# Another order of the weight chunks, o's low-rank part on VectorE, low-rank rows split and stacked through DRAM

## Chip, cores and metric

One NeuronCore of a Trainium2 chip runs the whole program. The metric is the device time of one execution in microseconds (us), of which the median of several runs is given. Engines are named as in the profile: PE is TensorE, DVE is VectorE, ACT is ScalarE, POOL is GpSimd, SP is SyncE, which here only issues DMAs.

## What is computed

Four stages on a tensor of 1024 tokens by 512. The change touches the first. Its weights are NF4 codes (integers 0 to 15) with a scale for every 64 inputs, each with a low-rank addition:

```python
def _lin_lora(x, W, A, B):
    return x @ W.T + (x @ A.T) @ B.T          # rank 16
q, k, v = (_lin_lora(x, dequant(codes_attn[i], scales_attn[i]), A_h[i], B_attn[i]) for i in range(3))
attn = (q + k + v) / 3.0
o = _lin_lora(attn, dequant(codes_attn[3], scales_attn[3]), A_h[3], B_attn[3])
x1 = x + o
g = _lin_lora(x1, dequant(codes_gu[0], ...), A_h[4], B_gu[0])
u = _lin_lora(x1, dequant(codes_gu[1], ...), A_h[5], B_gu[1])
d = _lin_lora(silu(g) * u, dequant(codes_down, ...), A_down, B_down)
return x1 + d                                # then x = layernorm(x + this)
```

(The code above is the reference in short.) x is 2 x 512 x 512, the hidden width is 1792. After it come a quantised 512 x 512 layer with a rank 64 addition, an attention layer with one head of 128, and a layer of 64 rank-16 experts of which 16 are taken, each with a residual and a layer norm.

## The kernel before

Weights are handled in **chunks** of 128 x 512. `chunk_list` (L111) gives their order: four of o, then q, k, v of slice 0, of slice 1, 2, 3, then g and u of hidden tiles 0 and 1, d 0 and d 1, then g, u, d of the further tiles. A chunk is looked up from its codes by piecewise lines: ACT makes four planes (`low` two of them, L785; `mid`, L807; `out`, the top one, L785) and DVE joins them in four steps (L1316 low, L1322 mid, L1329 clip, L1338 value). POOL multiplies the value by its scale (L718, for q, k, v L723) into `wf`, a ring of three. Codes come through a ring of three as well: SP issues the code of chunk j only when the top plane of chunk j-3 is made (L658).

Since q, k, v and o are linear, they are folded: per slice i of 128 inputs the sum of the three weights is made in the PSUM bank `acc_ps` (low-rank products L1049, then fp32 products with a scaled unit matrix L1052, L1055), split by ACT and DVE into a high and a low part (`acc`; `wq_hi`, `wq_lo`), and multiplied with o's weight (`wo_hi`, `wo_lo`) in twelve matmuls plus three times the unit matrix (L1069). The result is the matrix `m1`, again split (`m1_hi` by ACT, `m1_lo` by DVE). `partial(i, r)` (L1027) adds slice i's share of x1 = m1 x for the first 512 tokens to bank r; the other 512 tokens follow as four products of twelve matmuls. All products are made in three matmuls, high x high, high x low, low x high (`product`, L991).

o's four chunks go through PE too: for each, the low-rank product (L1037) and an fp32 product with the unit matrix (L1040), whose bank ACT and DVE split.

x1 is split into `x1_hi`, `x1_lo` (ACT, DVE), and DVE adds it to x in `xs`. Then the **units**: unit n is a hidden tile f = n // 2 and a half b of the tokens, a gate and an up product of twelve matmuls each. For g, u and d chunks PE makes the low-rank product in the bank `lora_ps` (`lora`, L1000; the same bank as `acc_ps`, so each waits for `lora_added` of the one before), DVE adds it to `wf` (`merge`, L1353), ACT and POOL split (`split`: `gu_hi` L780, `gu_lo` L740). `res(t)` (L1137) transposes a token tile of xs, which ACT copies to `rows`; the down products are added there by DVE (L1413).

The low-rank rows of g and u lie in the 128 rows of `la_gu` and `lb_gu` three times over (high, low, high), so that one matmul gives all three products. They are loaded from DRAM already stacked; ACT makes the high part of all rows (`bprep`) and DVE the low part of one band (L1306). For d the same is `dprep`, after x1.

Each engine runs one hand-written order: `vector_order` (L135) for ACT, DVE and POOL together, in which `half(c, 0)` is mid and clip of a chunk and `half(c, 1)` is low of the next chunk and out; `tensor_order` (L251) for PE's units. Work that is queued behind a waiting instruction of its engine waits too.

## Time and profile before

| | |
|---|---|
| median of 3 runs | 535.43 us (533.67 to 535.5) |
| profiled execution, its own time | 534.0 us |
| its span | 532.1 us |
| mean granted clock of PE | 0.993 |
| PE matmul busy | 494.5 us (93%) |
| DVE busy | 379.4 us (71%) |
| ACT busy | 293.9 us (55%) |
| POOL busy | 251.6 us (47%) |

The profile is of one execution. Busy time is the time in which an engine has an instruction at work. The granted clock is a share of full speed, of PE alone. In a timeline each line is an instruction, or some merged of one kind: start, duration, engine and line, what it writes and reads, how many, and in square brackets how long the engine was idle before it and what it waited for. Ends of matmuls are modelled, so their starts are the safer numbers. A wait for several things is put down to the last to come.

### The profile page before, as it was taken

What the parts mean: (1) busy time and instruction counts of PE and PEld (TensorE: products, weight loads), DVE (VectorE), ACT (ScalarE), POOL (GpSimd) and SP (SyncE); (2) the same over time, 40 slices, a digit from 0 to 9 for tenths busy, and PEclk for the clock granted to TensorE, in tenths of its full rate; (3) what the DMA queues carried; (4) which work ended last, traced back from release to release, by engine and by line L of the source; (5) the groups of instructions that cost most, each with busy time, mean ns of one, the idle gap of its engine ahead of it and who ended that gap; (6) DMA issues with size and microseconds to landing.
All of it is one profiled execution on the core that took longest, in us unless ns stands there. A gap on an engine that the chain in (4) does not pass through costs nothing.

```text
span 532.1 us, 7568 instructions
## 1 busy us (share of the span) xinstructions
PE 494.5 (93%) x2278; PEld 394.7 (74%) x2278; DVE 379.4 (71%) x716; ACT 293.9 (55%) x541; POOL 251.6 (47%) x252
## 2 busy tenths in 40 slices
PE   2968999788999999999999999899998899999995
PEld 0236678567888888888888888688886788888874
DVE  4888898666789789797987983577457966366442
ACT  6688856676666576666674742158487422332021
POOL 3357702465566576665674753147479410110001
PEclk9999999899999999999999999999999999999998
DMA  6575421243233333343333300740000000000011
GB/s 169 173 263 159 139 59 41 79 139 100 80 106 75 96 105 118 82 119 97 105 115 97 103 19 0 267 155 5 1 1 1 2 2 19 21 20 22 0 41 39
DMA packets 21415, 43.01 MB, mean 81 GB/s; under 512 B 3328, under 2 KB 3456, under 8 KB 21120
## 3 DMA queue, kind: packets, MB, share of 16 engines
q1 hardware_dynamic: 21152, 42.15, 25.6%
q0 software_dynamic: 224, 0.38, 0.3%
q8 instruction: 19, 0.31, 0.2%
q14 instruction: 20, 0.16, 0.1%
HBM read 40.42 MB, written 2.10 MB: 80 GB/s over the span
## 4 chain that ended last, share of the span: by engine, by line
PE 69%; ACT 3%; issue 3%; DVE 2%; POOL 0%; POOLq 0%; ACTq 0%; DVEq 0%
PE bank L996 62%; PE bank L1162 3%; PE bank L1009 2%; PE bank L1266 1%; ACT prob L957 1%; ACT pT_hi L780 1%; PE bank L1018 0%; DVE rmax L1480 0%; DVE pT_lo L1306 0%; ACT eb_hi L780 0%; ACT bank L785 0%; DVE rows L1413 0%; POOL gu_lo L740 0%; ACT v_hi L780 0%; PE bank L1025 0%
## 5 line engine op out<-in xcount | busy, mean ns | idle before, releaser
L718 POOL TENSOR_TENSOR wf<-value,scale 128x512 f32<-128x512 f32 x50 | 64.5, 1290 | 93.1 <-DVE value L1338 93.1
L996 PE MATMUL bank<-x_hi,gu_hi 128*128 128x512 f32 x224 | 89.9, 401 | 1.7 <-POOL gu_lo L740 1.7
L996 PE MATMUL bank<-x_lo,gu_hi 128*128 128x512 f32 x224 | 88.2, 394 | 0.0
L996 PE MATMUL bank<-x_hi,gu_lo 128*128 128x512 f32 x224 | 88.1, 393 | 0.0
L763 POOL TENSOR_TENSOR rstd<-veps,neg_half 128x1 f32<-128x1 f32 x32 | 17.6, 549 | 121.8 <-issue 110.5
L785 ACT ACTIVATE bank<-code 128x512 f32<-128x512 int32 x124 | 68.7, 587 | 0.0
L1316 DVE SCALAR_TENSOR_TENSOR low<-bent,bank 128x512 f32<-128x512 f32 x62 | 42.5, 685 | 24.0 <-ACT bank L785 19.4
L746 POOL TENSOR_TENSOR h_lo<-act_f,h_hi 128x512 fp32r<-128x512 f32 x28 | 36.3, 1297 | 31.7 <-ACT h_hi L780 31.7
L1413 DVE SCALAR_TENSOR_TENSOR rows<-bank,rows 128x512 f32<-128x512 f32 x48 | 33.0, 688 | 24.7 <-PE bank L996 24.3
L996 PEld LDWEIGHTS bank<-x_hi,gu_hi 128*128 128x128 f32 x224 | 42.6, 190 | 9.9 <-issue 2.1
L996 PEld LDWEIGHTS bank<-x_hi,gu_lo 128*128 128x128 f32 x224 | 42.5, 190 | 9.1
L996 PEld LDWEIGHTS bank<-x_lo,gu_hi 128*128 128x128 f32 x224 | 42.6, 190 | 7.9
L1329 DVE SCALAR_TENSOR_TENSOR low<-low,bank 128x512 f32<-128x512 f32 x62 | 42.7, 688 | 6.9 <-DVE bank L1322 0.5
L780 ACT ACTIVATE h_hi<-act_f 128x512 fp32r<-128x512 f32 x28 | 17.7, 631 | 52.0 <-DVE act_f L1403 48.5
L996 PE MATMUL bank<-wd_hi,h_hi 128*128 128x512 f32 x112 | 44.2, 395 | 1.6 <-DVE rows L1413 1.6
L1322 DVE SCALAR_TENSOR_TENSOR bank<-code,bank 128x512 f32<-128x512 int32 x62 | 42.6, 686 | 1.6 <-ACT bank L807 1.6
L996 PE MATMUL bank<-wd_hi,h_lo 128*128 128x512 f32 x112 | 43.7, 390 | 0.0
L996 PE MATMUL bank<-wd_lo,h_hi 128*128 128x512 f32 x112 | 43.7, 390 | 0.0
L1338 DVE SCALAR_TENSOR_TENSOR value<-bank,low 128x512 f32<-128x512 f32 x62 | 42.4, 684 | 0.1
L785 ACT ACTIVATE bent<-code 128x512 f32<-128x512 int32 x62 | 38.5, 621 | 3.2 <-DMA code<-codes 3.2
L740 POOL TENSOR_TENSOR gu_lo<-wf,gu_hi 128x512 fp32r<-128x512 f32 x28 | 36.7, 1310 | 5.2 <-ACT gu_hi L780 4.8
L918 ACT ACTIVATE rows<-rows,nbias,rstd 128x512 f32<-128x512 f32 x24 | 19.3, 812 | 35.7 <-POOL nbias L766 35.6
(198 smaller groups left out, 1172.7 us busy)
## 6 DMA issues: line engine op xcount, KB each, us to landing
code<-codes SPq DMA_DIRECT2D x62, 256.0 KB, 2.7
scale<-scales SPq DMA_DIRECT2D x100, 128.0 KB, 3.0
xs<-xT SPq DMA_DIRECT2D x2, 1024.0 KB, 5.6
ea_raw<-ex_A SPq DMA_DIRECT2D x1, 2048.0 KB, 9.9
eb_raw<-ex_B SPq DMA_DIRECT2D x1, 2048.0 KB, 7.5
out<-rows SPq DMA_DIRECT2D x8, 256.0 KB, 2.0
bgu_raw<-loB_gu SPq DMA_DIRECT2D x1, 896.0 KB, 4.7
wqkv_raw<-w_qkv SPq DMA_DIRECT2D x1, 768.0 KB, 4.3
```

Of the source, the lines that this page charges most:

```text
L718: pool.tensor_tensor(w, v, scale[:, i % RING_CODES, :], ALU.mult).then_inc(scaled_done, 1)
L740: pool.tensor_tensor(lo, shaped(c, w), hi.bitcast(F32), ALU.subtract).then_inc(lo_done, 1)
L746: pool.tensor_tensor(h_lo[:, f % RING_H, hs], act_f[:, n % 2, :], h_hi[:, f % RING_H, hs].bitcast(F32), ALU.subtract).then_inc(hlo_done, 1)
L780: nc.scalar.activation(dst, src, ACT.Copy).then_inc(done, 1)
L785: nc.scalar.activation(dst, src, ACT.Prelu, bias=float(start), scale=float(slope), alpha=float(alpha)).then_inc(done, 1)
L918: nc.scalar.activation(rows[:, t, :], src, ACT.Identity, bias=nbias[:, s:s + 1], scale=rstd[:, s:s + 1]).then_inc(norm_done, 1)
L996: last = nc.tensor.matmul(ps, a, b, start=start and i == 0 and n == 0, stop=stop and i == len(terms) - 1 and n == 2)
L1316: nc.vector.scalar_tensor_tensor(low[:, j % 2, :], bent[:, j % 2, :], float(BEND_LOW[3] - BEND_LAST[3]), last_ps[:, :], ALU.add, ALU.min). ...
L1322: nc.vector.scalar_tensor_tensor(mid_ps[:, :], code[:, j % RING_CODES, :], float(CODE_SHIFT), mid_ps[:, :], ALU.add, ALU.max).then_inc(mid ...
L1329: nc.vector.scalar_tensor_tensor(lj, lj, float(BEND_LAST[3]), mid_ps[:, :], ALU.add, ALU.min)\
L1338: nc.vector.scalar_tensor_tensor(value[:, j % 2, :], top_ps[:, :], float(BEND_TOP[3]), low[:, j % 2, :], ALU.add, ALU.max).then_inc(value_ ...
L1413: nc.vector.scalar_tensor_tensor(rows[:, t, :], down_bank(gi, t)[:, :], 1.0 / GAIN, rows[:, t, :], ALU.mult, ALU.add).then_inc(down_added, 1)
```

## The change

- **Order of the chunks.** q, k, v of slice 0, then the four of o, then q, k, v of slices 1 to 3, then as before. In `vector_order` the first sixteen chunks take fixed extras ahead of clip, ahead of out and after out, from three tables.
- **o.** The four low-rank products of o run after slice 0's, ahead of slice 0's sums, and end in their own banks. The products with the unit matrix are gone. DVE adds the low-rank product to `wf` (`merge`), and ACT and POOL split it as they do for g. m1 of slice 0 has its own bank, and m1 is scaled by 1 / (3 GAIN).
- **Scaled unit matrices** are made by POOL instead of ACT, and the scales of q, k, v come through SP's queue behind the first code instead of POOL's.
- **x.** It is loaded in eight tiles, each with its own semaphore, ahead of the codes of o 3 to k 3.
- **Low-rank rows of g, u, d.** They are loaded once each, spread over 128 partitions (576 and 352 columns), split there by ACT and POOL (`spread`), written to DRAM as high and low, and read back into the stacked rows: `stack_gu` (2 stores, a wait, 9 loads) ahead of v 3's code, `stack_d` (2 stores, a wait, 12 loads) ahead of g 1's. The stacked buffers are zeroed first (DVE, POOL). `bprep` and `dprep` are gone.
- **x1 and rows.** `xs` now gets x1 alone, by ACT for tiles other than 5 and 7 and by DVE for these. `rows` is loaded with x ahead of d 1's code, and DVE adds the transposed x1 to it (`res`), which ACT copied before.
- **Low-rank products of g and u.** g 0 after the first partial of slice 3, u 0 after the last, g 1 and u 1 after the second and third product of the other tokens. The res steps begin one place later.

```diff
-    chunks = [("o", k) for k in range(KT)] + [(m, i) for i in range(KT) for m in "qkv"]
+    chunks = [(m, 0) for m in "qkv"] + [("o", k) for k in range(KT)]
+    chunks += [(m, i) for i in range(1, KT) for m in "qkv"]
...
+X1F_ON_V = (5, 7)
+
+BEFORE_CLIP = {
+    ("o", 2): [("acc", 0)], ("o", 3): [("merge", ("o", 1)), ("split", ("o", 1))],
+    ("q", 1): [("merge", ("o", 2)), ("split", ("o", 2))],
+    ("q", 2): [("m1", 0)], ("k", 2): [("acc", 1)], ("k", 3): [("acc", 2)],
+}
+BEFORE_OUT = {
+    ("o", 2): [("merge", ("o", 0)), ("split", ("o", 0))], ("q", 1): [("merge", ("o", 3))],
+    ("v", 2): [("m1", 1)], ("v", 3): [("m1", 2)],
+}
+AFTER_OUT = {
+    ("q", 1): [("split", ("o", 3))], ("k", 1): [("xsplit", 0)], ("v", 1): [("spread", 0)], ("q", 2): [("xsplit", 1)],
+    ("k", 2): [("spread", 1)], ("v", 2): [("xsplit", 2)], ("q", 3): [("xsplit", 3)], ("v", 3): [("xsplit", 4)],
+}
...
+        c = CHUNKS[j]
+        order.append(("mid", c))
+        order += BEFORE_CLIP.get(c, [])
+        order += [("clip", c), ("low", CHUNKS[j + 1])]
+        order += BEFORE_OUT.get(c, [])
+        order.append(("out", c))
+        order += AFTER_OUT.get(c, [])
...
+    order += [("acc", 3), ("xsplit", 5)]
+    half(("u", 0), 0)
     due.clear()
-    order += [("acc", 2 * KT - 1), ("bprep", 0), ("bprep", 1), ("m1", KT - 1)]
-    half(("u", 0), 0)
+    order.append(("xsplit", 6))
     half(("u", 0), 1)
     due.clear()
-    order += [("x1", 0), ("x1", 1), ("x1", 2), ("x1", 3), ("merge", ("g", 0)), ("x1", 4), ("split", ("g", 0))]
+    order += [("m1", 3), ("xsplit", 7)]
     half(("g", 1), 0)
-    order += [("x1", 5), ("merge", ("u", 0))]
+    order += [("x1", 0), ("merge", ("g", 0)), ("split", ("g", 0)), ("x1", 1), ("x1", 2), ("x1", 3)]
     half(("g", 1), 1)
-    order += [("x1", 6), ("split", ("u", 0)), ("x1", 7), ("dprep", 0)]
+    order += [("merge", ("u", 0)), ("split", ("u", 0)), ("x1", 4)]
+    due.clear()
     half(("u", 1), 0)
+    order += [("x1", 5), ("merge", ("g", 1)), ("split", ("g", 1))]
     half(("u", 1), 1)
+    order += [("x1", 6), ("merge", ("u", 1)), ("split", ("u", 1)), ("x1", 7)]
+    due.clear()
     half(("d", 0), 0)
-    order += [("silu", 0), ("res", 0)]
+    order.append(("silu", 0))
     half(("d", 0), 1)
     unit_h(0)
-    order.append(("res", 1))
+    order.append(("res", 0))
     half(("d", 1), 0)
-    order += [("silu", 1), ("res", 2)]
+    order += [("silu", 1), ("res", 1)]
     half(("d", 1), 1)
     unit_h(1)
-    order.append(("res", 3))
+    order.append(("res", 2))
...
+            def stack_gu():
+
+                sp.wait_ge(spreadhi_done, 1)
+                sp.wait_ge(spreadlo_done, 1)
+                sp.wait_ge(zeroed_v, 2)
+                cols = spread_cut(0)
+                sp.dma_start(scratch_hi[:, cols], spread_hi[:, cols].bitcast(F32)).then_inc(scratch_in, 16)
+                sp.dma_start(scratch_lo[:, cols], spread_lo[:, cols].bitcast(F32)).then_inc(scratch_in, 16)
+                sp.wait_ge(scratch_in, 32)
+                for i in range(3):
+                    a, b = (scratch_lo if i == 1 else scratch_hi), (scratch_lo if i == 2 else scratch_hi)
+                    for g in range(2):
+                        r = 32 * i + RANK * g
+                        sp.dma_start(long(la_gu[r:r + RANK, g, :].bitcast(F32)), wide(a[64 * g:64 * g + 64, 0:P]))\
+                            .then_inc(gu_rows_in, 16)
+                    sp.dma_start(long(lb_gu[32 * i:32 * i + 32, :].bitcast(F32)), wide(b[:, P:SPREAD_GU])).then_inc(gu_rows_in, 16)
...
+            def stack_d():
+
+                sp.wait_ge(spreadhi_done, 2)
+                sp.wait_ge(spreadlo_done, 2)
+                sp.wait_ge(zeroed_p, 2)
+                piece = FF // 2 // PIECES
+                cols = spread_cut(1)
+                sp.dma_start(scratch_hi[:, cols], spread_hi[:, cols].bitcast(F32)).then_inc(scratch_in, 16)
+                sp.dma_start(scratch_lo[:, cols], spread_lo[:, cols].bitcast(F32)).then_inc(scratch_in, 16)
+                sp.wait_ge(scratch_in, 64)
+                for i in range(3):
+                    a, b = (scratch_lo if i == 1 else scratch_hi), (scratch_lo if i == 2 else scratch_hi)
+                    for g in range(2):
+                        r, half = 64 * g + RANK * i, slice(64 * g, 64 * g + 64)
+                        sp.dma_start(long(la_dp[r:r + RANK, :].bitcast(F32)), wide(a[half, SPREAD_GU:SPREAD_GU + piece]))\
+                            .then_inc(d_rows_in, 16)
+                        sp.dma_start(long(lb_dp[r:r + RANK, g, :].bitcast(F32)), wide(b[half, SPREAD_GU + piece:]))\
+                            .then_inc(d_rows_in, 16)
...
+                if c in x_before:
+                    k, tk = x_tile(x_before[c])
+                    sp.dma_start(xs[:, k, tk], xT[:, k, tk]).then_inc(x_in[x_before[c]], 16)
+                if c == ("q", 2):
+                    sp.dma_start(spread[:, spread_cut(0)], lora_gu).then_inc(spread_in[0], 16)
+                    sp.dma_start(spread[:, spread_cut(1)], lora_d).then_inc(spread_in[1], 16)
+                if c == ("v", 3):
+                    stack_gu()
+                if c == ("g", 1):
+                    stack_d()
+                if c == ("d", 1):
+                    sp.wait_ge(gu_rows_in, 16 * 9)
+                    sp.wait_ge(d_rows_in, 16 * 12)
+                    for b in range(NB):
+                        sp.dma_start(rows[:, b * TPB:(b + 1) * TPB, :], x_rows[:, b * TPB:(b + 1) * TPB, :])\
+                            .then_inc(x_rows_in, 16)
...
+                    if n not in X1F_ON_V:
+                        act.wait_ge(xlo_done, KT * (b + 1))
+                        copy(xs[:, o, b * SEQ:(b + 1) * SEQ], mm_ps[n % 4][:, :], x1f_done)
...
+            pe.wait_ge(lora_in, 32)
+            slice_lora(0)
+            pe.wait_ge(olora_in, 32)
+            for k in range(KT):
+                nc.tensor.matmul(mm_ps[k][:, :], la_o[:, k * P:(k + 1) * P], lb_o[:, :], start=True, stop=True)\
+                    .then_inc(olora_ready, 1)
+            pe.wait_ge(gain_set, 3)
+            slice_sums(0)
+            pe.wait_ge(acchi_done, 1)
+            pe.wait_ge(acclo_done, 1)
+            slice_lora(1)
+            slice_m1(0)
+            for i in range(1, KT):
+                if i > 1:
+                    pe.wait_ge(m1hi_done, i)
+                    pe.wait_ge(m1lo_done, i)
+                    slice_lora(i)
+                slice_sums(i)
+                pe.wait_ge(m1hi_done, i)
+                pe.wait_ge(m1lo_done, i)
+                pe.wait_ge(xhi_done, i)
+                pe.wait_ge(xlo_done, i)
+                partial(i - 1, 0)
+                partial(i - 1, 1)
+                slice_m1(i)
+                partial(i - 1, 2)
+                partial(i - 1, 3)
...
+                if r == 0:
+                    lora(("g", 0))
+            lora(("u", 0))
 
             pe.wait_ge(xhi_done, 2 * KT)
             pe.wait_ge(xlo_done, 2 * KT)
             for n in range(KT, NB * KT):
                 r = n - KT
-                pe.wait_ge(x1hi_done, n - 3)
-                pe.wait_ge(xs_done, n - 3)
+                pe.wait_ge(x1lo_done, n - 3)
+                pe.wait_ge(x1f_done, x1f_before(n - 3))
                 cut = slice(r * P, (r + 1) * P)
                 product(mm_ps[r][:, :], [(m1_hi[:, k, cut], m1_lo[:, k, cut], x_hi[:, k, SEQ:], x_lo[:, k, SEQ:])
                                          for k in range(KT)]).then_inc(x1_ready, 1)
-                if r in (1, 3):
-                    lora((("u", 0), ("g", 1))[r // 2])
+                if r in (1, 2):
+                    lora((("g", 1), ("u", 1))[r - 1])
...
+                    if c[0] == "o":
+                        dve.wait_ge(olora_ready, c[1] + 1)
+                        nc.vector.scalar_tensor_tensor(w, mm_ps[c[1]][:, :], GAIN, w, ALU.mult, ALU.add)\
+                            .then_inc(o_merged, 1)
+                        continue
...
+                elif kind == "res":
+                    t = item[1]
+                    dve.wait_ge(res_ready, t + 1)
+                    dve.wait_ge(x_rows_in, 16 * NB)
+                    nc.vector.tensor_tensor(rows[:, t, :], bank[7][:, :], rows[:, t, :], ALU.add).then_inc(res_set, 1)
```

## Rows read from the trace of the kernel before

**Rows 1.** Waits of PE up to 140 us; line waited for: us, times, longest

```profile
PE bank L1037 <- DMA lb_qkv<-loB_qkv: 10.2, 1, 10.2
PE bank L1052 <- POOL wf L728: 3.5, 1, 3.5
PE bank L1146 <- ACT rows L780: 3.5, 1, 3.5
...
PE bank L1009 <- DVE wf L1353: 1.8, 2, 1.4
PE bank L996 <- POOL gu_lo L740: 1.7, 1, 1.7
```

**Rows 2.** Busy time by engine in stretches; granted clock, DMA share, GB/s last

```profile
97.10:101.40 4.30, 4.27 (x17) 3.52 (x18) 3.21 (x6) 3.22 (x7) 1.64 (x3) 0.62 0.45 122
130.00:170.00 40.00, 40.00 (x188) 33.48 (x187) 33.51 (x51) 24.67 (x46) 23.57 (x18) 1.00 0.30 86
```

**Rows 3.** Timeline of PE; start, duration, instruction, idle before and releaser

```profile
10.19 2.07 PE L1037 MATMUL bank<-lb_o,la_o 16*128 16x512 f32 x2 [10.19 <-DMA lb_qkv<-loB_qkv]
12.19 2.08 PE L1040 MATMUL bank<-wf,unit_eye 128*128 128x512 f32 x2
...
26.22 2.07 PE L1049 MATMUL bank<-la_qkv,lb_qkv 48*128 48x128 f32 x8
...
37.12 0.77 PE L996 MATMUL bank<-wo_hi,wq_hi 128*128 128x512 f32 x1 [1.50 <-DVE wq_lo L1306]
...
71.84 0.47 PE L996 MATMUL bank<-x_hi,m_hi 128*128 128x512 f32 x1
```

**Rows 4.** Timeline of PE later; first gate product, ninth product

```profile
87.53 0.44 PE L996 MATMUL bank<-x_hi,gu_hi 128*128 128x512 f32 x1
...
127.39 0.47 PE L996 MATMUL bank<-x_hi,gu_hi 128*128 128x512 f32 x1 [1.75 <-POOL gu_lo L740]
```

**Rows 5.** Timeline of DVE; start, duration, instruction, idle before and releaser

```profile
5.03 0.69 DVE L1316 SCALAR_TENSOR_TENSOR low<-bent,bank 128x512 f32<-128x512 f32 x1 [3.84 <-ACT bank L785]
...
18.94 0.69 DVE L1306 TENSOR_TENSOR wo_lo<-bank,wo_hi 128x512 fp32r<-128x512 f32 x1 [0.26 <-ACT wo_hi L780]
...
28.02 0.69 DVE L1316 SCALAR_TENSOR_TENSOR low<-bent,bank 128x512 f32<-128x512 f32 x1 [0.37 <-ACT bank L785]
28.62 0.68 DVE L1338 SCALAR_TENSOR_TENSOR value<-bank,low 128x512 f32<-128x512 f32 x1
...
30.61 0.68 DVE L1316 SCALAR_TENSOR_TENSOR low<-bent,bank 128x512 f32<-128x512 f32 x1
...
61.21 0.69 DVE L1338 SCALAR_TENSOR_TENSOR value<-bank,low 128x512 f32<-128x512 f32 x1
...
68.88 2.02 DVE L1306 TENSOR_TENSOR lb_gu<-bgu_raw,lb_gu 32x1792 fp32r<-32x1792 f32 x1 [0.38 <-ACT lb_gu L780]
71.05 0.69 DVE L1367 SCALAR_TENSOR_TENSOR m_lo<-bank,m_hi 128x512 fp32r<-128x512 f32 x1
```

**Rows 6.** Timeline of ACT in the o chunks

```profile
18.31 0.60 ACT L780 ACTIVATE wo_hi<-bank 128x512 fp32r<-128x512 f32 x1 [1.37 <-PE bank L1040]
18.80 0.62 ACT L785 ACTIVATE bent<-code 128x512 f32<-128x512 int32 x1
19.32 1.11 ACT L785 ACTIVATE bank<-code 128x512 f32<-128x512 int32 x2
```

**Rows 7.** Timeline of SP's DMA issues

```profile
28.90 0.43 SPq L644 DMA_DIRECT2D bgu_raw<-loB_gu  x1
29.37 0.42 SPq L645 DMA_DIRECT2D agu_raw<-loA_gu  x1
```

**Rows 8.** DMA issues by tile; KB each, median us from issue to landing

```profile
code<-codes SPq DMA_DIRECT2D x62, 256.0 KB, 2.7
...
out<-rows SPq DMA_DIRECT2D x8, 256.0 KB, 2.0
```

**Rows 9.** Waits of SP's queue, whole span

```profile
SPq L658 <- ACT bank L785: 125.1, 58, 6.7
```

More of the change, by code:

```diff
@@ L124 @@
 MERGED = [c for c in CHUNKS if c[0] not in "qkvo"]
-SPLIT = MERGED
+SPLIT = [c for c in CHUNKS if c[0] not in "qkv"]
 SCALED = [c for c in CHUNKS if c[0] not in "qkv"]
@@ L155, in half @@
         if part == 1:
-            if c[0] == "o":
-                due.append([3, ("acc", c[1])])
-            elif c[0] == "v":
-                due.append([3, ("acc", KT + c[1])])
-                due.append([6, ("m1", c[1])])
-            elif c[0] not in "qk":
-                due.append([2, ("merge", c)])
-                due.append([3, ("split", c)])
+            due.append([2, ("merge", c)])
+            due.append([3, ("split", c)])
         due.sort(key=lambda x: x[0])
@@ L591, in weight_wait, with x_tile, spread_cut, x1f_before @@
             engine.wait_ge(scaled_done, CHUNKS.index(c) + 1)
-        def acc_bank(a):
-            return mm_ps[a] if a < KT else acc_ps
-        def acc_dest(a):
-            hi, lo = (wo_hi, wo_lo) if a < KT else (wq_hi, wq_lo)
-            return hi[:, a % KT, :], lo[:, a % KT, :]
+        def x_tile(i):
+            return i % KT, slice(i // KT * SEQ, (i // KT + 1) * SEQ)
+        def spread_cut(i):
+            return (slice(0, SPREAD_GU), slice(SPREAD_GU, SPREAD_GU + SPREAD_D))[i]
+        def x1f_before(n):
+            return sum(i not in X1F_ON_V for i in range(n))
+        def m1_bank(i):
+            return mm_ps[3] if i == 0 else acc_ps
         def dest(c):
             kind, k = c
+            if kind == "o":
+                return wo_hi[:, k, :], wo_lo[:, k, :]
             if kind in "gu":
```

267 lines of the change are left out of this document (109 added, 158 removed).

## The prediction

> **What bounds the kernel now.** I read the waits of PE first, because PE is busy 93% of the span, and then the stretches. From 130 us on PE has no gap (40.00 of 40.00 us busy in the stretch from 130 to 170, at granted clock 1.00 [rows 2]), while DVE is at 33.5. What the change touches lies ahead of that, so a microsecond taken from the time at which PE enters that unbroken stretch is a microsecond off the end. The waits of PE up to 140 us are the stock to draw on [rows 1]: 10.2 for the first low-rank rows, 3.5 for a summed slice, and in the unit stage 3.5 (a transpose of xs waiting for ACT's copy of rows), 1.8 (two low-rank products waiting for a merge) and 1.7 (gu_lo). The first of these three also costs clock: after it PE runs 4.3 us at a granted 0.62 [rows 2]. In the o chunks PE is no idle engine but the bound: each chunk needs two fp32 products of 2.0 us (starts 10.19, 12.19 [rows 3], eight of them until 26.22), so a chunk takes 4.0 us, although DVE and ACT can turn one out in 2.59 (two "low" steps at 28.02 and 30.61 [rows 5]). I use four marks on PE: first m1 product 37.12, first product of partial(3) 71.84 [rows 3], first gate product 87.53, ninth unit product 127.39 [rows 4]. After the last of them the work is the same in both kernels.
>
> **Constants of the hand-off.** An ACT copy is seen by DVE 0.63 after its start (18.31, 18.94 [rows 5, 6]); ACT steps follow each other at 0.52 (18.80, 19.32 [rows 6]); DVE steps at 0.60 (28.02, 28.62), and a DVE step is 0.69 long, after which ACT goes on, so 0.72 from its start (my reading of 0.69 plus a hand-off); DVE to PE takes 0.79 (71.05 to 71.84 [rows 3, 5]). With these I followed the new order item by item on each queue.
>
> **1. Opening, to the first m1 product: +0.9 us.** Codes of q, k, v need no scale rows, so the second code lands earlier and the chunks run at 2.59 from about 7.0. DVE stands ready for the new acc 0, which sits after mid of o2, at 19.2. PE does not: its two qkv low-rank rows are now second and third on POOL's queue, so it starts near 7.0 instead of 10.2, but then has 2.0 (slice 0) + 8.0 (four o low-rank products) + 4.0 (two sums) in line, to 21.4. So acc 0 holds DVE and, in its own order, ACT for 2.9 us. What is queued behind is the whole of o2, o3 and q1. From there each chunk carries a merge on DVE and a split on ACT, and ACT's split waits for the merge (0.72 after its start) with the next chunk's low and top steps behind it: about 3.4 us a chunk. The last o split leaves POOL at 38.0, against 37.12 [rows 3]. DVE's number of steps is the same (four merges replace four wo_lo steps; four splits of 1.3 us go to POOL, which is under half busy). The zeroing on DVE is 2816 elements a row; at the 2.02 us of 1792 [rows 5] it is 3.2 us, and DVE idles 3.84 before its first look-up step at 5.03 [rows 5]. That on POOL and the three eyes there (at most 6 us at 1.3 us for 512) end by 10, before PE's first sum needs them. If the two rows land as late as now (10.2), PE reaches acc 0 3 us later: bound +4; if they land by 6, it is 0.
>
> **2. Slices 1 to 3 without any late code: -2.8 us.** The spacing of m1_lo was 9.7, 9.7 and 9.2; in the new order, where steps between mid and clip fill the gap of 0.2 and slice 1's product has no transfer from o in front, I get 7.7, 9.1 and 8.9. Steps 1 and 2 together put partial(3) at 69.9 against 71.84 [rows 3]: **-1.9**. The value of v3 starts at 60.9 against 61.21 [rows 5], so the gain is small: the chain v3, acc, m1, partial is not shortened. The two low-row splits that stood on DVE there (one took 2.02 at 68.88 [rows 5]) hid behind PE's m1 product; their removal lets DVE finish u0's look-up earlier, which step 5 uses.
>
> **3. The trips through DRAM on SP's queue: +5.0 us.** This is the new wait. stack_gu stands before the code of v3: two stores, a wait for both, nine row transfers. An issue costs 0.42 to 0.43 on SP, 0.47 apart [rows 7]; I take 0.43. A 256 KB store lands in 2.0, a code in 2.7 [rows 8]. For two stores of 295 KB I take 2.3 from the second's issue. SP gets past the code of k3 when its slot's top step is done, at 48.4; stores issued by 48.9, landed 51.2, rows issued 55.1, code of v3 landed 57.8. ACT wants it at 55.6: **2.2** late, and nothing in ACT's order behind low(v3) can pass it. stack_d stands before the code of g1: code and scales of u0 are out at 61.1 (the code waits for k3's top step, itself late by then), stores landed 63.9, twelve rows until 69.1, code landed 71.8. In ACT's order m1 3 stands behind low(g1) and out(u0), so it comes 1.6 after that, at 73.4, where PE's product has it ready at 70.6: **2.8** more. Who waits: DVE's m1_lo and all of PE (partial(3)). Bounds: nothing if ACT wants both codes 2 to 3 us later than I place them, 8.3 if an issue is 0.55 and a store 2.7. The large load of x rows before d1's code waits only for what has landed, and d1's code is wanted 9 us later: nothing.
>
> The Trainium skill says of a DMA (page DMA: Bandwidth & Descriptors, section Anatomy of one DMA) that about 2.0 us of it are fixed, most of that the receipt of the last write, longest where the target is HBM, and that bytes come on top at 436 GB/s. The trace's 2.0 for a store to HBM [rows 8] is at or under that; by the rule the two stores would land after 2.7, and the sum would be 0.8 us higher.
>
> **4. x1, from partial(3) to the first gate: +3.1 us, and 0.3 for the clock.** The xs additions (8 steps of DVE) become 6 copies on ACT and 2 on DVE. Four low-rank products instead of three now stand in here, each waiting for the merge of the one before. Following DVE and ACT: merge u0 is done 0.7 after PE wants it, and merge g1 (behind x1 4, mid, clip and both steps of x1 5) 2.4 after. So 3.1 over the present 15.7. PE is idle about 3 us in front of partial(3); after 3.5 us at 93.7 it fell to the low level [rows 1, 2]; I take 0.3, bounds 0 and 1.6 (4.3 us x 0.38).
>
> **5. Units, first gate to ninth product: -7.2 us.** Gone: the waits 3.5, 1.8 and 1.7 [rows 1], the clock 4.3 x 0.38 = 1.6 [rows 2], and the product of u1's rows, 0.5, now in step 4: 9.1. The 3.5 goes because merges and splits of g1 and u1 are done in step 4, and ACT no longer has to copy rows between them; DVE adds them instead (8 steps of 0.6, and DVE has 6 us of slack in 40 [rows 2]). What is late next is the same chain one step on: merge g2 before u2's product (1.0) and u2's split before the ninth product (0.9). Net 9.1 - 1.9.
>
> **Sum:** -1.9 + 5.0 + 0.3 + 3.1 - 7.2 = -0.7. On the profiled execution: 534.0 - 0.7 = 533.3. That execution lies 1.4 under the median of 535.4, which I take as the base: 535.4 - 0.7 = 534.7 us. A change of 0.5%, 2.7 us, is about what a measurement of this kernel can tell from none.
>
> **Rivals.**
> A. *The codes are not late.* If the row transfers are cheap enough, or ACT is further back than I place it, step 3 is zero: -5.7, 529.7 us. For it: SP waits at nearly every code now, 125.1 us in 58 times [rows 9], and the 3-deep ring leaves about 4.5 us between the slot of v3 coming free for the queue and the last moment for its code. Against it: stack_gu alone is 6.7 us of issues and a round trip. With it goes the case that the x1 waits are shorter than 3.1 (merges found earlier), also worth 2 to 3.
> B. *The trips cost more, and PE cools.* Place: the code of g1. Issues at 0.55 and stores at 2.7 make step 3 8.3 instead of 5.0, and PE is then idle over 3.5 us before partial(3), as long as the gap that dropped its clock [rows 1, 2], so 1.6 instead of 0.3: +3.9, 539.3 us, slower. It decides from about 0.52 us an issue upward.
> C. *The o part does not get faster.* If the low-rank rows land as late as now, acc 0 waits 3 us longer and the moved o work buys nothing: +2.4, 537.8 us. It counts as no change, at its edge. Against it: the six scale transfers of the first three chunks are gone from the queues at that time.
>
> **How the numbers follow.** Forecast and C within 0.5%: 0.34 and 0.08. A: 0.36. B: 0.22. The range reaches nearly to A with its x1 part (528) and to B (540). So faster 0.36, same 0.42, slower 0.22.
>
> **What will show it.** Step 1: o chunks at 2.6 with one DVE idle of about 3 us for the acc around 20, first m1 product near 38. Step 2 and 3: ACT idle, released by the DMA of code, twice, near 56 and 70; the first of partial(3) near 75 rather than 72. If those two idles are missing, A holds, and partial(3) starts by 70. Step 4: PE idle for DVE wf twice, 0.7 and 2.4, first gate near 94. Step 5: no transpose waiting 3.5, granted clock 1.00 from the first gate on, ninth product near 127. I am wrong in mechanism if SP's wait before the rows is longer than 4 us, if PE waits for the stacked rows themselves (its low-rank products, not ACT, released by DMA), or if the unbroken stretch after the ninth product breaks up because DVE, which now adds eight rows, falls behind.

## The result, and the profile after

| | before | after |
|---|---|---|
| median, runs side by side | 534.55 us | 541.76 us (540.99 to 542.83) |
| ratio after to before | | 1.0136 [1.0106, 1.0166] |
| span of the profiled execution | 532.1 us | 539.2 us |

The changed kernel is 7.2 us slower. The forecast was 534.7 us, no change, and its range ended at 540, so the time lies outside the range. The marks say where the forecast left the road:

| mark on PE | before | forecast | after |
|---|---|---|---|
| first m1 product | 37.12 | 38.0 | 36.81 |
| first product of partial(3) | 71.84 | 75.2 | 82.63 |
| first gate product | 87.53 | 94.0 | 102.42 |
| ninth unit product | 127.39 | 126.7 | 134.47 |

(The forecast of a mark is its time before plus the terms of the sum up to it: 71.84 - 1.9 + 5.0 + 0.3 = 75.2, and so on. Before: [rows 3, 4].) The error at the ninth product is 7.8 us, 7.4 of it there already at partial(3). Nearly all that went wrong lies between 37 and 83 us; behind that the x1 stage came 1.0 longer than forecast and the unit stage 0.6 shorter.

Timeline of PE after, at the marks and at the two long gaps:

```profile
36.81 0.77 PE L1072 MATMUL bank<-wo_hi,wq_hi 128*128 128x512 f32 x1 [14.17 <-POOL wo_lo L832]
...
65.98 0.77 PE L1114 MATMUL bank<-la_qkv,lb_qkv 48*128 48x128 f32 x2 [5.90 <-DVE m_lo L1468]
...
82.63 0.77 PE L1072 MATMUL bank<-x_hi,m_hi 128*128 128x512 f32 x1 [5.31 <-issue]
...
102.42 0.39 PE L1072 MATMUL bank<-x_hi,gu_hi 128*128 128x512 f32 x1
...
134.47 0.47 PE L1072 MATMUL bank<-x_hi,gu_hi 128*128 128x512 f32 x1 [0.84 <-POOL gu_lo L832]
```

The gap of 14.17 answers to PE's idle time in the o chunks and is no loss, because the first m1 product came a little earlier than before. The gaps of 5.90 and 5.31 are new. Going back one engine at a time from them, DVE had stood still for 5.97 and 6.22, and ACT before it, for a code. (The profile names no releaser for the gap of 5.31. DVE's m_lo starts at 81.85, 0.78 before PE goes on; that hand-off took 0.79 in the kernel before.) First the waits of ACT up to 140 us, then the two instructions of ACT and what DVE did after them:

```profile
ACT bent L877 <- DMA code<-codes: 13.9, 4, 6.2
```

```profile
60.74 0.63 ACT L877 ACTIVATE bent<-code 128x512 f32<-128x512 int32 x1 [6.16 <-DMA code<-codes]
...
79.43 0.63 ACT L877 ACTIVATE bent<-code 128x512 f32<-128x512 int32 x1 [5.99 <-DMA code<-codes]
```

```profile
61.95 0.69 DVE L1413 SCALAR_TENSOR_TENSOR low<-bent,bank 128x512 f32<-128x512 f32 x1 [5.97 <-ACT bent L877]
...
80.64 0.69 DVE L1413 SCALAR_TENSOR_TENSOR low<-bent,bank 128x512 f32<-128x512 f32 x1 [6.22 <-ACT bank L877]
...
81.85 0.68 DVE L1468 SCALAR_TENSOR_TENSOR m_lo<-bank,m_hi 128x512 fp32r<-128x512 f32 x1
```

These are the codes of v3 and g1, the two in front of which `stack_gu` and `stack_d` stand. SP's queue shows why they are late (timeline of the queue; two issues of before stand in [rows 7]):

```profile
47.22 0.37 SPq L687 DMA_DIRECT2D scratch_hi<-spread_hi  x1
47.63 0.42 SPq L688 DMA_DIRECT2D scratch_lo<-spread_lo  x1
51.21 1.28 SPq L694 DMA_DIRECT2D la_gu<-scratch_hi  x2
52.53 0.59 SPq L696 DMA_DIRECT2D lb_gu<-scratch_hi  x1
...
57.06 1.85 SPq L743 DMA_DIRECT2D code<-codes  x2
...
64.05 0.52 SPq L705 DMA_DIRECT2D scratch_hi<-spread_hi  x1
64.61 0.43 SPq L706 DMA_DIRECT2D scratch_lo<-spread_lo  x1
68.27 0.59 SPq L712 DMA_DIRECT2D la_dp<-scratch_hi  x1
68.92 0.58 SPq L714 DMA_DIRECT2D lb_dp<-scratch_hi  x1
...
76.41 0.53 SPq L743 DMA_DIRECT2D code<-codes  x1
```

The first block holds the queue from 47.22 to 57.06, 9.8 us: 4.0 for the stores and the wait for them, 5.85 for nine row loads. The second holds it from 64.05 to 76.41, 12.4 us: 4.2 and 8.1 for twelve. Row loads are mostly 0.64 apart; a single one comes 1.01 behind the one before it. The waits of SP and the DMA issues of the page give the rest:

```profile
SPq L712 <- DMA scratch_lo<-spread_lo: 3.2, 1, 3.2
```

```profile
scratch_hi<-spread_hi SPq DMA_DIRECT2D x1, 288.0 KB, 3.3
scratch_lo<-spread_lo SPq DMA_DIRECT2D x1, 288.0 KB, 3.6
...
la_dp<-scratch_hi SPq DMA_DIRECT2D x4, 56.0 KB, 2.4
```

And the stretches of PE (columns as in [rows 2]):

```profile
51.20:57.00 5.80, 5.54 (x24) 3.65 (x23) 4.44 (x8) 3.38 (x7) 4.58 (x4) 1.00 0.43 108
66.00:71.00 5.00, 5.00 (x13) 3.09 (x13) 2.92 (x5) 1.54 (x3) 3.54 (x3) 0.54 0.25 76
82.60:88.00 5.40, 5.37 (x15) 4.48 (x16) 2.67 (x4) 2.23 (x5) 2.36 (x3) 0.53 0.71 175
102.40:134.40 32.00, 30.36 (x152) 24.83 (x150) 26.58 (x42) 20.27 (x38) 19.09 (x15) 1.00 0.42 116
140.00:180.00 40.00, 40.00 (x188) 33.43 (x188) 33.71 (x52) 25.22 (x48) 25.21 (x20) 1.00 0.32 88
```

After each of the two new gaps PE runs about 5 us at a granted clock of 0.53 or 0.54, the lower of its two levels (1.2 GHz). The unit stage, which was 39.9 us long, is now 32.05 and runs at clock 1.00; the unbroken stretch behind it is as it was. Behind the ninth product nothing is added: 134.47 against 127.39 is 7.1, and the spans differ by 7.1.

### The profile page after: what moved, and what is told of

The parts are those of the page before. It is cut to its first block, busy times and chain, and to the rows that moved or that the text cites. A ratio compares the mean times of both kernels' runs of the same rounds, so it can differ in the third digit from the quotient of the medians.

```text
span 539.2 us, 7600 instructions
## 1 busy us (share of the span) xinstructions
PE 487.9 (90%) x2270; PEld 394.9 (73%) x2270; DVE 377.4 (70%) x716; ACT 288.6 (54%) x534; POOL 262.3 (49%) x262
## 4 chain that ended last, share of the span: by engine, by line
PE 68%; issue 3%; ACT 3%; DVE 2%; POOL 0%; POOLq 0%; ACTq 0%; DVEq 0%
PE bank L1072 61%; PE bank L1257 3%; PE bank L1085 2%; PE bank L1361 1%; ACT prob L1033 1%; ACT pT_hi L872 1%; PE bank L1094 0%; DVE rmax L1573 0%; DVE pT_lo L1403 0%; ACT eb_hi L872 0%; DVE rows L1506 0%; POOL gu_lo L832 0%; ACT v_hi L872 0%; PE bank L1100 0%; PE bank L1101 0%
## 5 line engine op out<-in xcount | busy, mean ns | idle before, releaser
L877 ACT ACTIVATE bank<-code 128x512 f32<-128x512 int32 x124 | 68.9, 587 | 0.0
L1413 DVE SCALAR_TENSOR_TENSOR low<-bent,bank 128x512 f32<-128x512 f32 x62 | 42.4, 684 | 23.7 <-ACT bent L877 10.2
L872 ACT ACTIVATE h_hi<-act_f 128x512 fp32r<-128x512 f32 x28 | 17.7, 632 | 54.6 <-DVE act_f L1491 52.8
L899 ACT ACTIVATE bank<-code 128x512 f32<-128x512 int32 x62 | 36.6, 591 | 3.5 <-DVE low L1426 3.5
```

The costliest lines, as they stand in the source:

```text
L872: nc.scalar.activation(dst, src, ACT.Copy).then_inc(done, 1)
L877: nc.scalar.activation(dst, src, ACT.Prelu, bias=float(start), scale=float(slope), alpha=float(alpha)).then_inc(done, 1)
L899: nc.scalar.activation(mid_ps[:, :], code[:, j % RING_CODES, :], ACT.Relu, bias=float(RELU_MID[1]), scale=float(RELU_MID[0])).then_inc(mid ...
L1413: nc.vector.scalar_tensor_tensor(low[:, j % 2, :], bent[:, j % 2, :], float(BEND_LOW[3] - BEND_LAST[3]), last_ps[:, :], ALU.add, ALU.min). ...
```

## The experiments

Ratios are to the kernel before, run on the same chip beside each kernel, since that kernel's own median moved between 533.4 and 535.6 us. For sums I turn a ratio into microseconds on 534.6: after is +7.3.

**Theory and rivals.** Theory Q: SP's queue holds the codes of v3 and g1 back, and this is the whole loss. Rivals: the round trip (stores and their wait) is what costs; the stack's traffic disturbs the other transfers; the new order of the chunks loses time by itself.

### Without the stack

```diff
                 if c == ("v", 3):
-                    stack_gu()
+                    pass
                 if c == ("g", 1):
-                    stack_d()
+                    pass
```

(The waits of PE and SP for the rows go with it; the rows stay zero, so the low-rank part of g, u and d is left out of the result. DVE zeroes all of lb_gu instead of 32 of its rows, which takes 1.55 us either way. The same holds for the next run and for the one with two of three portions.)

> The changed kernel without the two trips through DRAM: no stores, no row loads; the stacked rows stay zero, so the low-rank part of g, u and d is left out of the result while its matmuls and merges still run. Theory Q (SP's queue makes the codes of v 3 and g 1 late, and this is the whole loss): ACT's two idles of about 6 us for codes are gone, the first product of partial(3) starts near 69 instead of 82.6, the first gate near 88, the ninth product near 120, time about 527 us, some 7 below the kernel before. Theory O (the order itself loses: merges and splits on ACT and DVE give back what the o part saves): time 534 or more, even with no code late. Theory B (memory traffic of the trips slows every landing): also about 527, so this run does not tell it from Q.

Ratio 0.9912 [0.988, 0.9943]: -4.7 us to before and 12.0 less than the changed kernel. The median of 529.9 lies 2.9 above the expected 527, though the gaps went as expected. Waits of PE up to 140 us:

```profile
PE bank L1084 <- DVE wf L1453: 3.6, 3, 2.2
...
PE bank L1071 <- POOL gu_lo L831: 0.8, 1, 0.8
```

The gaps of 5.9 and 5.3 are gone and only the waits for merges remain. So what the changed kernel has besides the stack doesn't lose; it gains, and the stack costs 12. The first m1 product is at 37.16 and partial(3) starts at 70.15.

### Stores and their wait only

```diff
                 sp.wait_ge(scratch_in, 32)
-                for i in range(3):
-                    a, b = (scratch_lo if i == 1 else scratch_hi), (scratch_lo if i == 2 else scratch_hi)
-                    for g in range(2):
...
```

(The same in `stack_d`. The low-rank part of g, u and d is again left out.)

> The changed kernel with the four stores and both waits for them, but no row loads (the low-rank part of g, u and d is left out, as zero rows). Theory Q: SP is held 4.0 us before the code of v 3 and 4.2 us before that of g 1, about what the three-deep ring has to spare, so codes are at most 0.5 us late each: 527.5 to 528.5 us. Theory R (the round trip to HBM is what costs, the loads are cheap): most of the loss stays, 535 us or more.

0.9897 [0.9862, 0.9933]: the same as without the stack, and with a median of 530.1 some 1.6 above the expected 527.5 to 528.5. The round trip holds the queue for about 4 us twice, yet after 17 us ACT never waits for a code: the ring of three codes has that much in hand. The rival of the round trip alone falls.

### Stores earlier, row loads in place

```diff
+                if c == ("k", 3):
+                    store(0, scratch_in)
                 if c == ("v", 3):
                     stack_gu()
+                if c == ("g", 0):
+                    store(1, scratchd_in)
```

(The stores are taken out of the two blocks, and d's get a semaphore of their own.)

> The changed kernel, complete, with the stores of g and u issued one code earlier and those of d two codes earlier, so that SP finds them landed; the 21 row loads stay where they are. Theory Q: SP is held 5.9 and 8.1 us instead of 9.9 and 12.4, codes of v 3 and g 1 are late by about 2.2 and 4: 533 to 535 us. Theory R: about 528. Theory B (same bytes at nearly the same time): 540 to 542.

1.0009 [0.9987, 1.003]: +0.5, that is 6.8 less than the changed kernel with the same transfers, as expected. ACT waits 3.4 and 2.95 for the two codes instead of 6.2 and 6.0. So round trip and row loads add up in one queue. The round trip alone cost nothing (the run before). The row loads alone still cost 5.2 over the kernel without the stack, and behind the round trip their whole length comes on top of what the ring can cover.

### Row loads in portions, each behind a code

```diff
+                if c == ("k", 3):
+                    store(0, scratch_in)
+                if c == ("v", 3):
+                    store(1, scratchd_in)
+                    rows_gu(0)
+                if c == ("g", 0):
+                    rows_gu(1)
+                if c == ("u", 0):
+                    rows_gu(2)
+                if c == ("g", 1):
+                    rows_d(0)
...
```

(These lines stand behind the issue of the chunk's code, `rows_gu(i)` issues three loads, `rows_d(i)` four; all the work is done.)

> The changed kernel, complete, with the same stores and row loads cut into portions of three or four and issued behind the codes of k 3, v 3, g 0, u 0, g 1, u 1 and d 0 instead of in two blocks ahead of v 3 and g 1. Theory Q: no code late by more than 0.5 us, all rows landed before their first use, time within 1.5 us of the kernel without trips, about 528. Theory B: the bytes are the same, so codes are still late and the time is 538 or more. If the low-rank products of g 0 wait for their rows instead, PE shows a wait for la_gu or lb_gu near 70 us.

0.9889 [0.9854, 0.9924]: 528.96 us, -5.9, faster than both kernels, with the same bytes, the same stores and the same 21 row loads. So traffic isn't the cause of the loss, though it may have a small part in it: a code issued directly behind row loads is used later than the 2.7 of [rows 8], here 3.7 (57.90) and 4.1 (61.94) after its issue, and both of these were waited for. A part of SP's queue, and the two waits that are left on ACT:

```profile
50.50 0.33 SPq L738 DMA_DIRECT2D code<-codes  x1
...
52.14 1.28 SPq L698 DMA_DIRECT2D la_gu<-scratch_hi  x2
53.47 0.59 SPq L700 DMA_DIRECT2D lb_gu<-scratch_hi  x1
54.16 0.53 SPq L738 DMA_DIRECT2D code<-codes  x1
```

```profile
54.47 0.62 ACT L887 ACTIVATE bent<-code 128x512 f32<-128x512 int32 x1
...
57.90 0.63 ACT L887 ACTIVATE bent<-code 128x512 f32<-128x512 int32 x1 [1.28 <-DMA code<-codes]
...
61.94 0.63 ACT L887 ACTIVATE bent<-code 128x512 f32<-128x512 int32 x1 [0.87 <-DMA code<-codes]
```

v3's code goes out at 50.50, not 57.06, and ACT takes it at 54.47 without a wait.

### One block alone

From the kernel with the portions, first d's stores and loads put back as one block ahead of g1's code, then gu's ahead of v3's:

```diff
                 if c == ("g", 1):
+                    stack_d()
...
-                if c == ("g", 1):
-                    rows_d(0)
```

```diff
                 if c == ("v", 3):
+                    stack_gu()
...
                 if c == ("v", 3):
                     store(1, scratchd_in)
-                    rows_gu(0)
```

> Complete kernel. The rows of g and u travel between the codes as in e4_rows_between, but d's two stores and its 12 row loads stand as one block ahead of g1's code. Theory Q (SP's queue holds the codes back, one block at a time, each block with its own price): SP should be held for about 12.4 us from about 61.6, as in the changed kernel's second block; the code of g1 would land near 77 where ScalarE wants it near 65.7 and m1 is whole by 68.4. ScalarE should show one wait on a code of 6 to 9 us, partial(3) should start about 7 to 9 us behind e4's 69.8, and the clock should fall in the gap: 536.5 to 539 us against 529.0 for e4. A rival, that the two blocks of the changed kernel cost half of its loss each, gives 535.4. If the loss came with gu's block alone, this run would stay at 529.

> Complete kernel. gu's two stores and its nine row loads stand as one block ahead of v3's code, and d's rows travel between the codes as in e4_rows_between. Theory Q: the code of v3 lands 6 us late as in the changed kernel (ScalarE's wait of about 6.2 near 60.7), the product m1 part 2 follows it late, and the codes behind are in time again: 529.0 + 6.2 + about 1 for TensorE's clock after the gap = about 536 us. If the later codes had slack enough to take the delay in, it would be 530 to 532.

d's block alone: 1.0097 [1.0064, 1.013], +11.1 over the kernel with portions. gu's alone: 1.0066 [1.0038, 1.0095], +9.5. Both (the changed kernel): +13.2. They don't add, and both came out above their expectations: 540.3 against 536.5 to 539, and 538.3 against 536. ACT with d's block alone:

```profile
65.97 0.62 ACT L896 ACTIVATE x_hi<-xs 128x512 fp32r<-128x512 f32 x1
78.45 0.63 ACT L901 ACTIVATE bent<-code 128x512 f32<-128x512 int32 x1 [11.86 <-DMA code<-codes]
```

11.86 us late in one piece, against 6.16 + 5.99 in two. The block ends at nearly the same time either way: the code of g1 goes out at 75.34 here and at 76.41 in the changed kernel. What differs is when ACT asks for it: the delay of v3's code has already pushed ACT back by 6. A late transfer is only as late as its reader is early, so of these two blocks in one queue the second costs only what the first has not already cost.

With gu's block alone ACT waits 5.60 for v3's code, near the expected 6.2, and the kernel still loses 9.5. Much of the rest is PE's clock. PE's timeline there, the same place with the portions, and two stretches with gu's block:

```profile
66.76 2.04 PE L1136 MATMUL bank<-la_qkv,lb_qkv 48*128 48x128 f32 x8 [5.61 <-DVE m_lo L1490]
...
71.52 1.01 PE L1094 MATMUL bank<-x_hi,m_hi 128*128 128x512 f32 x1
```

```profile
60.55 1.13 PE L1124 MATMUL bank<-la_qkv,lb_qkv 48*128 48x128 f32 x8 [0.47 <-DVE m_lo L1478]
...
63.02 0.79 PE L1082 MATMUL bank<-x_hi,m_hi 128*128 128x512 f32 x1
```

```profile
66.00:72.00 6.00, 5.24 (x13) 3.29 (x13) 3.79 (x7) 2.83 (x6) 3.74 (x4) 0.50 0.49 123
...
90.00:99.00 9.00, 6.77 (x25) 5.17 (x25) 6.05 (x10) 4.40 (x9) 3.20 (x3) 0.83 0.29 97
```

The sums of slice 3 and what precedes them take 4.76 (66.76 to 71.52) where the kernel with portions needs 2.47 (60.55 to 63.02), because they run at a granted 0.50 after the idle 5.61. Of the 10.3 us between the ninth products of the two profiled executions (131.23 and 120.93), 5.3 lie in the slices with the late code, 2.3 in the slow sums, 1.5 in the x1 stage (20.6 instead of 19.1, with its stretch at 0.83), 0.9 in a later first m1 product and 0.3 elsewhere. Only the first two are shown to come from the block. The stage of 20.6 is none of its own: it is 20.7 in the profiled executions of the kernel with stores only, which has no late code, and of the one with early stores, at granted clocks below 1.00 there too (0.84 and 0.81). The expectation had allowed 1 us for the clock.

### Each block one code later

```diff
-                if c == ("v", 3):
+                if c == ("g", 0):
                     stack_gu()
-                if c == ("g", 1):
+                if c == ("u", 1):
                     stack_d()
```

> Complete kernel: the changed kernel with each block of the stack, otherwise as it is, one code later in SP's queue: gu's ahead of g0's code, d's ahead of u1's. Theory Q: what costs time is a code wanted soon behind a block. From e4_rows_between ScalarE wants g0 at 61.1 and u1 at 76.7; a block from 48.2 holds SP to about 58.1, the code of g0 lands near 61.5 (0.5 to 1 late), a second block from about 64.6 to 77 lets the code of u1 land near 80, 3 to 4 late, part of it under the x1 stage's slack. So 530 to 533 us, 9 to 12 less than the changed kernel with the same instructions. The rival, that the length of the blocks counts and not their place, gives 541.8.

1.0091 [1.0063, 1.0119], +4.9: the expectation of 530 to 533 missed. It is 2.4 less than the changed kernel, and the two intervals just overlap. ACT:

```profile
56.00 0.58 ACT L899 ACTIVATE bank<-code 128x512 f32<-128x512 int32 x1
64.26 0.63 ACT L877 ACTIVATE bent<-code 128x512 f32<-128x512 int32 x1 [7.68 <-DMA code<-codes]
```

I had read the time at which ACT wants g0's code from the wrong row: 61.1 is where it wants u0's. It wants g0's at 56.6, only 2.1 after v3's, because no work stands between these two look-ups in ACT's order. So moving gu's block by one code wins nothing: ACT waits 7.68 for g0's code. Moving d's block takes its wait away: u1's code goes out at 80.34, ACT takes it at 86.11 and there is no wait on it. The time is that of gu's block alone, within the intervals. The blocks are as long as before; what changed is how soon behind each of them the reader wants a code.

### Two of three portions

```diff
-                for i in range(3):
+                for i in range(2):
```

(In both blocks, and the counts waited for with them. The third portion of the rows stays zero, so a part of the low-rank products is left out of the result.)

> Leaves out a part of the computation: the third portion of the stacked rows (high of one factor with low of the other) of g, u and d stays zero; 3 of 9 and 4 of 12 row loads aren't issued, the rest of the changed kernel is as it is. It asks for the slope. Theory Q: SP's blocks end 1.9 and 1.9 + 2.7 us sooner at 0.64 us a load; the code of g1 goes out at about 71.9 instead of 76.4, and the time follows it one for one: 541.8 - 4.5 = 537.3, less up to 1 of the clock's loss: 536.3 to 537.5. If SP were not what holds the time, this run would stay at 541 to 542.

1.007 [1.0047, 1.0092], +3.7: 3.5 less than the changed kernel, where 4.3 to 5.5 less was expected. (The median itself is 536.64; it was run beside a kernel before of 533.43.) In the profiled executions g1's code goes out at 72.20 instead of 76.41, 4.2 earlier, and the ninth product comes at 129.43 instead of 134.47, 5.0 earlier. So the time follows the release of SP's queue about one for one; the ratios and the traces don't settle it more closely. Part of the 5.0 is the stage from partial(3) (78.28) to the first gate (97.39), 19.1 again, where the changed kernel needs 19.8.

### The merge of g1 ahead of the sixth x1 tile

In the kernel with the portions:

```diff
-    order += [("x1", 5), ("merge", ("g", 1)), ("split", ("g", 1))]
+    order += [("merge", ("g", 1)), ("split", ("g", 1)), ("x1", 5)]
```

> Complete kernel: e4_rows_between with the merge and split of g1 ahead of the sixth x1 tile in VectorE's and ScalarE's order. In e4 TensorE waits 2.2 us for g1's merged weights near 85.6. Theory: that wait is on the path and shrinks to about 1, while the x1 tile has slack: about 1.0 us less than e4, 528.0. Rival: the ninth product waits for the chain of look-ups behind it anyway and gives the gain back: the same as e4, 529.0, with the wait of 2.2 gone from the list and the ninth product still at 120.9.

0.9877 [0.985, 0.9905], which can't be told from 0.9889. In the profiled execution the wait did go from 2.23 to 1.03 and partial(3) to gate became shorter by about as much, but the first m1 product stood 1.0 later there (37.76 against 36.75) and codes landed later. Whether half a microsecond is won stays open.

### ACT makes the rows of x1

```diff
-                    nc.vector.tensor_tensor(rows[:, t, :], bank[7][:, :], rows[:, t, :], ALU.add).then_inc(res_set, 1)
+                    copy(rows[:, t, :], bank[7][:, :], res_set)
```

(From VectorE's program to ScalarE's, in the kernel with the portions. The residual x in x1 is left out of the result.)

> The result leaves out one part of the computation: the residual x in x1 (ScalarE copies the transposed x1 into rows where VectorE added x to it). It asks why the wait of 3.5 us of TensorE for the row form of x1 went. Theory: the early merges of u0 and g1 made it go, and it doesn't matter which of the engines makes the rows: within 0.7 us of e4, 529.0. Rival: VectorE doing it is what took the wait away, since ScalarE is busy with splits there: the wait returns in part, 531 to 532.5.

0.994 [0.9918, 0.9962]: 2.7 us more than with the portions, at 531.4 to 531.6 within the rival's range of 531 to 532.5. But the rival's mechanism isn't what one sees: the wait of 3.5 of before [rows 1] doesn't come back. In its place the merges and splits behind ACT's copies come later: PE waits 0.46 and 1.36 for merges (0.87 with the portions) and 1.31 for the split ahead of the ninth product (0.83 with the portions), and the unit stage is 33.7 instead of 32.0. So giving the rows to DVE is worth 1.6, and it isn't what made the wait of 3.5 go. That the early merges of step 4 did is what remains; no run takes them away alone. The other microsecond isn't shown to come from this edit. In the profiled executions it lies ahead of the stage, where PE ran more products at the slow pace (last section), and three kernels whose edits don't touch that place show the same.

## Why the prediction was wrong

**Step 1, the opening, +0.9: slightly too high.** Measured -0.3. PE began at 7.56 (forecast 7.0, before 10.2), its o products took 7.2 rather than 8.0 and DVE stood 1.55 for acc 0, not 2.9. The four merges of o came at 22.48, 25.61, 29.92 and 33.03, 3.5 apart where I had 3.4. Across all the kernels with this opening the first m1 product lies between 36.74 and 37.76, so much of the difference is no more than what one of these kernels differs from the next. The zeroing on DVE took 0.91 and 1.55, and a look-up step followed at 4.76, so it cost nothing, as said. Rival C, that the o part doesn't get faster, is out.

**Step 2, slices without a late code, -2.8: too large, and hidden by step 1.** With the portions partial(3) starts here:

```profile
69.80 0.47 PE L1082 MATMUL bank<-x_hi,m_hi 128*128 128x512 f32 x1
```

against 69.9 from steps 1 and 2. That agreement is luck. From the first m1 product to partial(3) it is 33.05 (69.80 - 36.75) against 34.72 before, so step 2 measured -1.7 instead of -2.8, and step 1 came 1.3 better than forecast. The kernel with the portions still has two short waits for codes, 1.28 and 0.87; without the stack partial(3) is at 70.15.

**Step 3, the trips through DRAM, +5.0: this is the step that failed.** Undisturbed it is 69.80, in the changed kernel 82.63: 12.8 us, beyond my upper bound of 8.3. The mechanism was the one I named, at both places: ACT stood idle for a code twice, from 54.6 and from 73.4 us. The size was wrong, in four terms. For v3's code:

| | forecast | measured |
|---|---|---|
| first store issued | 48.4 | 47.22 |
| from the second store's issue to the first row load | 2.3 | 3.58 (51.21 - 47.63) |
| nine row loads | 3.9 | 5.85 (57.06 - 51.21) |
| code's issue to its first use | 2.7 | 3.7 (60.74 - 57.06) |
| ACT wants the code | 55.6 | 54.58 (60.74 - 6.16) |
| late by | 2.2 | 6.16 |

Stores issued earlier give back 1.2, but 1.3 + 2.0 + 1.0 on the queue and 1.0 on the reader's side cost 5.3, so 2.2 became 6.2. For g1's code it is the same again. The block starts at 64.05 instead of 61.1, since the queue carries the first delay, stores and wait take 4.2 instead of 2.8, and twelve loads 8.1 instead of 5.2. So this code goes out at 76.4 where 69.1 was forecast, and is used at 79.4 where it was to land at 71.8. That is 7.6 late, the whole error at partial(3). (The forecast's 2.8 was the part that reaches PE; PE stood for 5.31, behind sums that had run slow.)

The largest term is the price of an issue: 21 row loads at 0.43 were to take 9.1 us and took 14.0, 4.9 more. The two stores and their wait, put at 2.3 from the second issue, took 3.6 and 3.7, 2.6 more for both. I had taken 0.43 from [rows 7], the issue of a plain load of rows, and even there the next issue comes 0.47 later. The loads from the scratch gather 64 or 128 pieces into 16 or 32 partitions, and one is 0.59 long and 0.64 apart from the next. The trace of before had a nearer row than the one I took, the two scale loads of a chunk on the same queue (timeline of SP before):

```profile
58.59 1.10 SPq L667 DMA_DIRECT2D scale<-scales  x2
```

That is 0.55 an issue, which I had as my upper bound. I had written that rival B decides from 0.52 us an issue upward. It did. The issue price was the number to widen, because it is multiplied by 21.

The Trainium skill says two things that bear on it. One (DMA: Bandwidth & Descriptors, section Anatomy of one DMA — SWDGE (gpsimd) path) is the section that the prediction drew on; it is written for POOL's path, and these transfers go by SP's, which the prediction didn't say. It lists descriptor generation as small and variable. If the length of an issue on SP is that, the gap between 0.43 and 0.64 is worth 21 x 0.21 = 4.4 us here and isn't small. Its 2.0 plus bytes at 436 GB/s gives an estimate of 2.7 for a store of 288 KB, and the rows show 3.3 and 3.6. The other statement of the Trainium skill (Perfetto Trace Analysis, section What "DMA-bound" means) is that a kernel is DMA-bound also when the issuing engine's track is solid DMA slices; the trace agrees: SP's track is solid from 51.21 to 57.06, while the DMA engines are busy for a share of 0.43 (the row 51.20:57.00).

**The clock, +0.3: under-sized too, though half hidden here.** I had put it at one place, in front of partial(3). PE fell to the low level there and also after the gap that ends at 66. In front of partial(3) (the row 82.60:88.00) the loss is 2.5 us at its face (5.4 x 0.47), yet the stage from partial(3) to the first gate is 19.8 against 19.1 with the portions: 0.7 reaches the path, since PE's waits for merges in that stage are 1.6 instead of 2.7. The loss at 66 is hidden behind the second late code in the changed kernel. With gu's block alone it isn't, and costs 2.3.

**Step 4, the x1 stage, +3.1: right.** With the portions 19.1 against 18.8 (it was 15.7 before); in the changed kernel 19.8. The two waits for merges were forecast at 0.7 and 2.4 and came at 0.46 and 2.23.

**Step 5, the units, -7.2: right.** -7.8 (39.86 to 32.05). What is late next was named as u2's merge, 1.0, and the split ahead of the ninth product, 0.9; PE waited 0.87 and 0.84. The 3.5, 1.8 and 1.7 are gone and the clock is 1.00 throughout.

**The rivals.** B's mechanism held, at its place and by its criterion, with a price above the one I gave: I had let the issue go to 0.55 and the store to 2.7, and 541.8 is above its 539.3 too. A is the time one gets when the codes aren't late (529.7 forecast; 529.9, 530.1 and 529.0 in the runs without lateness). Of my signs of a wrong mechanism none appeared: SP's wait for the stores was 3.2, not over 4, PE never waited for the stacked rows, and the stretch from 140 on has no gap.

So the opening, the slices, the x1 stage and the units were right within 1.3 us each, in part against each other, and step 3 was off by 7.8. The range was too narrow because its upper end, 8.3 for step 3, let only two terms go up, and neither far enough: 0.55 an issue was short by 2.4 us over both blocks, and 2.7 for the stores by 1.8. It gave nothing for a code that lands later behind other transfers, or for a reader that wants it earlier.

## What to carry to other kernels

In this kernel a block of issues in a queue cost its length less the prefetch in hand: 4 us of stores and wait cost nothing, and 9.8 us made a code 6.2 late. So write down for each transfer behind a block when its reader wants it, from the reader's own order, and put small portions behind the urgent ones: the same 21 loads cost about 13 us in two blocks and about nothing in portions. The delays of two blocks in the same queue didn't add. Price an issue from rows of the same shape in the same queue; where there is none, widen the range, above all for a price that is multiplied by 21.

## What the runs showed of the hardware

**Issues differ in length on the same queue.** Code 0.33, or 0.53 directly behind others; plain rows 0.42, and 0.47 from one to the next; scales 0.55; gathered rows 0.59, and 0.64 from one to the next, in portions of three as in blocks of twelve. Whether it is the shape alone is not shown: no run changes only that, and a load of 128 pieces (lb_gu, 0.59) is no longer than one of 64 (la_gu, 1.24 to 1.28 for two).

**PE can run its products at the slow pace while the granted clock reads 1.00.** In the kernel with ACT making the rows, PE idled 13.24 us ahead of the first m1 product and the stretch after it reads 1.00; in the changed kernel it idled 14.17 and the stretch reads 0.63. First the kernel with ACT's rows (stretches, then PE's timeline), then the changed one:

```profile
36.80:41.00 4.20, 3.45 (x8) 2.81 (x9) 4.10 (x8) 4.12 (x8) 3.06 (x4) 1.00 0.47 135
```

```profile
41.10 0.63 PE L1087 MATMUL bank<-wo_hi,wq_lo 128*128 128x512 f32 x1
41.53 0.63 PE L1087 MATMUL bank<-wo_hi,wq_hi 128*128 128x512 f32 x1
```

```profile
36.80:41.00 4.20, 4.19 (x12) 3.35 (x13) 4.00 (x7) 3.37 (x7) 3.19 (x3) 0.63 0.43 160
```

```profile
39.08 0.63 PE L1072 MATMUL bank<-wo_hi,wq_lo 128*128 128x512 f32 x1
39.51 0.58 PE L1072 MATMUL bank<-wo_hi,wq_hi 128*128 128x512 f32 x1
39.93 0.39 PE L1072 MATMUL bank<-wo_lo,wq_hi 128*128 128x512 f32 x1
```

In both, products start 0.43 apart at first and 0.23 apart later, nearly the ratio of the two levels, 1.2 and 2.4 GHz. Where the column says 1.00 all twelve of this product are slow, where it says 0.63 it is seven. The edit isn't the reason: the profiled executions with stores only, with early stores and with two of three portions also read 1.00 in this stretch, with the same idle of 13.24. The difference of five products at 0.20 is the microsecond by which the first m1 is finished later in the one (first m1_lo on DVE at 43.96 against 42.13, of which 0.74 is the later start). After an idle stretch the spacing of the products' starts is a safer reading of the pace than the column.
